# An attention and expert-layer kernel on one core: the softmax shift follows its scores by two query groups, the maxima go through TensorE in f16, and the output side moves by a group

## The reference

```
h   = layernorm(x)
q, k, v = h Wq + bq, h Wk + bk, h Wv + bv            # 16 heads of 16
s   = q.k / 4 + q.rel_emb[r - l + 511]  # 1024 x 1024 per head
x   = x + layernorm(softmax(s) v Wo + bo)
h   = layernorm(x)
w   = top 2 of softmax(h router_W + router_b), made to sum to 1
x   = x + layernorm(h base_W + base_b + shared + sum_e w_e B_e(A_e h))
```

## Time and profile before

| what | value |
|---|---|
| median of three runs | 6504.95 us (6501.69 to 6511.04) |
| profiled execution, its own time | 6501.09 us |
| its span, first to last instruction | 6499.3 us |
| mean granted TensorE clock, share of full | 0.99 |
| PE, weight loads, DVE, ACT, POOL busy | 95%, 89%, 77%, 48%, 56% |

### The profile page before, as it was taken

One profiled execution on the slowest core, in us unless ns is written; L12 is line 12 of the kernel. 1 busy time (PEld: TensorE's weight loads), 2 busy tenths in 40 slices (PEclk: granted clock), 3 DMA queues, 4 the chain that ended last, 5 costly groups with the idle time before them and its releaser, 6 DMA issues.

```text
span 6499.3 us, 408509 instructions
## 1 busy us (share of the span) xinstructions
PE 6203.9 (95%) x178176; PEld 5783.0 (89%) x178176; DVE 5036.1 (77%) x10289; ACT 3134.0 (48%) x5145; POOL 3640.9 (56%) x4707
## 2 busy tenths in 40 slices
PE   5999999999999999999999999999999999999997
PEld 4999899999999999999999999899999999998997
DVE  3777777777787777777777777777777777777776
ACT  2444444444444444444444444444444444444444
POOL 5555555555565555555555555555555555555555
PEclk8999999999999999999999999999999999999998
DMA  3111121111212112121111211112111121211210
GB/s 86 37 44 50 37 58 37 51 45 35 58 36 59 35 35 61 35 60 33 42 56 35 60 36 48 45 39 58 35 52 43 35 58 38 59 35 33 62 35 27
DMA packets 570089, 296.73 MB, mean 46 GB/s; under 512 B 384176, under 2 KB 534688, under 8 KB 568624
## 3 DMA queue, kind: packets, MB, share of 16 engines
q1 hardware_dynamic: 568624, 272.86, 15.2%
HBM read 184.46 MB, written 88.60 MB: 42 GB/s over the span
## 4 chain that ended last, share of the span: by engine, by line
PE 75%; DVE 15%; issue 6%; DVEq 3%; POOLq 1%; POOL 0%; SPq 0%; ACT 0%; DMA 0%
PE sc L665 19%; PE sc L681 13%; PE sc L660 11%; PE pw L691 11%; DVE r L960 6%; PE pm L672 6%; PE pm L712 4%; PE pw L698 4%; PE pw L712 4%; DVE nm L969 3%; DVE ceq L1008 2%; DVEq L971 2%; DVE y2n L926 1%; DVE dm L983 1%; PE pm L703 1%
## 5 line engine op out<-in xcount | busy, mean ns | idle before, releaser
L960 DVE TRANSPOSE_TENSOR_REDUCE r<-sc 128x32 f32<-128x1024 f32 x2048 | 2547.5, 1244 | 49.2 <-PE sc L665 48.3
L665 PE MATMUL sc<-rm,tw 96*128 96x32 f16 x65536 | 2288.9, 176 | 58.1 <-issue 58.1
L845 ACT ACTIVATE prob<-sc 128x1024 f32<-128x1024 f32 x2048 | 2095.7, 1023 | 237.9 <-PE sc L681 173.7
L665 PEld LDWEIGHTS sc<-rm,tw 96*128 96x128 f16 x65536 | 1976.9, 97 | 64.7 <-issue 64.3
L660 PE MATMUL sc<-qm,ks 96*128 96x64 f16 x32768 | 1635.2, 193 | 29.9 <-DMA ks<-qk_s 15.1
L969 DVE TENSOR_REDUCE nm<-pm 16x32 f16<-16x256 f32 x2048 | 840.5, 410 | 932.2 <-PE pm L672 931.4
L660 PEld LDWEIGHTS sc<-qm,ks 96*128 96x128 f16 x32768 | 1380.8, 98 | 105.7 <-issue 35.2
L681 PE MATMUL sc<-nmm,pick 128*128 128x64 f16 x32768 | 1305.7, 194 | 1.4 <-DVE nmm L972 1.4
L681 PEld LDWEIGHTS sc<-nmm,pick 128*128 128x128 f16 x32768 | 1150.9, 98 | 126.9 <-issue 103.2
L691 PE MATMUL pw<-prob,vs 128*32 128x128 f32 x32768 | 1110.2, 276 | 100.2 <-DVE nm L969 89.9
L691 PEld LDWEIGHTS pw<-prob,vs 128*32 128x32 f32 x32768 | 835.2, 110 | 158.5 <-DVE nm L969 119.8
(11 more groups left out here) (129 smaller groups left out, 5753.9 us busy)
## 6 DMA issues: line engine op xcount, KB each, us to landing
raw<-qk_s SPq DMA_DIRECT2D x774, 64.0 KB, 2.5
tw<-tw_s SPq DMA_DIRECT2D x512, 72.0 KB, 2.0
v_s<-vpad SPq DMA_DIRECT2D x136, 256.0 KB, 3.4
vs<-v_s SPq DMA_DIRECT2D x64, 512.0 KB, 3.7
ks<-qk_s SPq DMA_DIRECT2D x384, 64.0 KB, 2.4
xin<-x SPq DMA_DIRECT2D x138, 128.0 KB, 2.1
qk_s<-qkh SPq DMA_DIRECT2D x272, 64.0 KB, 1.7
qk_s<-qkl SPq DMA_DIRECT2D x272, 64.0 KB, 1.6
```

The lines of the kernel that those rows point to most:

```text
L665: last = mm(out3[:, :, 2 * k:2 * k + 2], tw[:, jp, u:u + P], rm[:, i, k, :, :], start=False, stop=False, skip_group_check=True)
L845: A(prob[:, jp % 2, :, :, i * IW:(i + 1) * IW], sc[:, 2 * buf:2 * buf + 2, :].rearrange("p c (h i) -> p c h i", i=IW), ACT.Exp).then_inc(s ...
L960: v.tensor_reduce(r1[:, :], sc[:, 2 * buf:2 * buf + 2, :].rearrange("p c (h i) -> p (c h) i", i=IW), axis=AX.X, op=ALU.max, apply_transpos ...
```

## The change

`LAG = 2` is new. In group `g` all that concerned group g-1 now concerns g-2, and the order on TensorE changes: first `transpose_max` of g-2, then `wide`, then the wait for `s_nmr`, `mixed`, the small `nm` matmul (when k is 2), and then scores of key block 0, the shift of g-2, scores of key block 1. On VectorE `spread` is that of g-2 and `maxima` that of g-1; on ScalarE the exp is that of g-2. The buffers remain three.

`r1` becomes f16 with 144 columns, of which 32 hold maxima; `transpose_max` is now a plain f16 matmul with 128 columns of `r1` as weights and a 128-column identity as the moving operand. Its output has 128 rows, of which VectorE reads 16. `nm` gets 128 rows, the unused ones zero, and its transpose has a place of its own in `pm`.

`wide` moves by a group: `transpose_parts` from k=3 to k=0 of the next stage, the projection's products from k=0 to k=1, `pv` from k=1 and k=2 to k=2 and k=3. `mixed` moves its transposes of `xn1` from g=0 to g=1 and of `o` from g=8 to g=9. ScalarE's copies move with them, and VectorE's `dm` goes from g=1 to g=3 and `o` from g=7 to g=8.

```diff
+LAG = 2
-        r1 = sb("r1", [P, 2 * H])
-        nm = sb("nm", [H, 2, P], f16)
+        r1 = sb("r1", [P, H + P], f16)
+        nm = sb("nm", [P, 2, P], f16)
...
-                    last = nc.tensor.transpose(p_max[:, c * P:(c + 1) * P], r1[:, c * H:(c + 1) * H], ident[:, :])
+                    last = mm(p_max[:, c * P:(c + 1) * P], r1[:, c * H:c * H + P], ident16[:, :], start=True, stop=True)
...
             def wide(t, n, g, att, proj, a):
-                if k and (a if jp == 0 else att):
-                    pj = (jp - 1) % NJP
-                    if k == 1:
-                        pe.wait_ge(s_exp, t * NG + g - 1)
...
-                        pv(pj, 0)
-                    elif k == 2:
-                        pv(pj, 1).then_inc(s_pv, 1)
-                    else:
-                        transpose_parts(t * NJP + jp - 1)
-                if k == 0 and jp < 3 and proj:
+                if k == 0 and (a if jp < 2 else att):
+                    transpose_parts(t * NJP + jp - 2)
+                if k == 1 and jp < 3 and proj:
...
+                if k >= 2 and (a if jp == 0 else att):
+                    pj = (jp - 1) % NJP
+                    if k == 2:
+                        pe.wait_ge(s_exp, t * NG + NI * jp)
...
+                        pv(pj, 0)
+                    else:
+                        pv(pj, 1).then_inc(s_pv, 1)
             def tile(t, n, att, proj, a, b, ph=None):
...
-                    old = a if g == 0 else att
+                    old = a if g < LAG else att
+                    count = t * NG + g - LAG + 1
+                    if read is not None:
+                        pe.wait_ge(*read)
+                    if k == 3 and (a if jp == 0 else att):
+                        pe.wait_ge(s_nmt, t * NJP + jp)
+                    if old:
+                        transpose_max(count)
+                    wide(t, n, g, att, proj, a)
+                    if old:
+                        pe.wait_ge(s_nmr, count)
+                    read = mixed(t, g, a, b)
+                    if k == 2 and (a if jp == 0 else att):
+                        mm(p_nm, nm[:, (jp - 1) % 2, :], ident16[:, 0:H], start=True, stop=True).then_inc(s_nmtp, 1)
...
                         scores(g, 0, buffer(ph, g))
-                    if read is not None:
-                        pe.wait_ge(*read)
                     if old:
-                        transpose_max(t * NG + g)
+                        shift(buffer(ph, g - LAG), count)
                     if att:
                         scores(g, 1, buffer(ph, g)).then_inc(s_scores, 1)
-
-                    wide_first = k == 1 or g in (0, 8)
-                    if wide_first:
-                        wide(t, n, g, att, proj, a)
-                    if old:
-                        pe.wait_ge(s_nmr, t * NG + g)
-                    read = mixed(t, g, att, a, b)
-                    if not wide_first:
-                        wide(t, n, g, att, proj, a)
-                    if old:
-                        shift(buffer(ph, g - 1), t * NG + g)
...
-                if g == 7 and a:
+                if g == 8 and a:
                     dve.wait_ge(s_osum, t)
...
-                        spread((g - 1) % NG, t * NG + g)
-                    if att:
-                        maxima(buffer(ph, g), t * NG + g + 1)
+                    if a if g < LAG else att:
+                        spread((g - LAG) % NG, t * NG + g - LAG + 1)
+                    if a if g < LAG - 1 else att:
+                        maxima(buffer(ph, g - LAG + 1), t * NG + g - LAG + 2)
```

More of the change, by code:

```diff
@@ L61, in sandwich_kernel @@
         ident = sb("ident", [P, P])
-        ident16 = sb("ident16", [H, H], f16)
+        ident16 = sb("ident16", [P, P], f16)
         pick = sb("pick", [P, H // 2, P], f16)
@@ L184, in sandwich_kernel @@
         pm = ctx.enter_context(nc.psum_tensor("pm", [P, 512], f32))
-        p_max = pm[0:H, 0:2 * P]
+        p_max = pm[:, 0:2 * P]
         p_n = pm[:, 2 * P:3 * P]
         p_t = pm[:, 2 * P:4 * P]
+        p_nm = pm[:, 4 * P - H:4 * P]
         s_const = sem("s_const")
@@ L503, in _ @@
             g.memset(nmm[:, :, :], 0.0)
+            g.memset(nm[:, :, :], 0.0)
+            g.memset(r1[:, :], 0.0)
             pool.drain()
@@ L510, in _ @@
             keep(ident[:, :], ALU.is_equal, 0, [[-1, P]], 1)
-            keep(ident16[:, :], ALU.is_equal, 0, [[-1, H]], 1)
+            keep(ident16[:, :], ALU.is_equal, 0, [[-1, P]], 1)
             half_h = H // 2
@@ L717, in both, with mixed @@
                 return [(lambda i, c=c: lhs[:, i, c, cols], lambda j, c=c: rhs[:, j, c, :]) for c in range(2)]
[L719 to L728, removed]
+            def mixed(t, g, a, b):
+                if g == 1 and b:
                     pe.wait_ge(s_xn1, t - 1)
@@ L736, in mixed @@
                     return s_hf, t - 1
-                if g == 8 and a:
+                if g == 9 and a:
                     pe.wait_ge(s_o, t)
@@ L758, in wide @@
                 jp, k = divmod(g, NI)
[L759 to L776 removed]
+                if k == 0 and (a if jp < 2 else att):
+                    transpose_parts(t * NJP + jp - 2)
+                if k == 1 and jp < 3 and proj:
+                    if a if jp < 2 else att:
                         pe.wait_ge(s_part, t * NJP + jp - 1)
@@ L792, in wide @@
                         product(pw[:, 0:D], *both(xT2, w_v2)).then_inc(s_vp, 1)
+                if k >= 2 and (a if jp == 0 else att):
+                    pj = (jp - 1) % NJP
+                    if k == 2:
+                        pe.wait_ge(s_exp, t * NG + NI * jp)
+                        pe.wait_ge(s_vs[pj], batch_of(t - 1 if jp == 0 else t) * 16 + 16)
+                        if proj and jp < 3:
+                            pe.wait_ge((s_xT, s_qkf, s_vf)[jp], n + 1)
+                        else:
+                            pe.wait_ge(s_part, t * NJP + jp - 1)
+                        pv(pj, 0)
+                    else:
+                        pv(pj, 1).then_inc(s_pv, 1)
             def tile(t, n, att, proj, a, b, ph=None):
@@ L849, in before @@
             def before(g, t, ph):
-                pg = (g - 1) % NG
-                exp(pg, buffer(ph, g - 1), t * NG + g, (t - 1 if g == 0 else t) * NJP + pg // NI - 1)
+                pg = (g - LAG) % NG
+                exp(pg, buffer(ph, g - LAG), t * NG + g - LAG + 1,
+                    (t - 1 if g < LAG else t) * NJP + pg // NI - 1)
             def tile(t, n, att, proj, a, b, ph=None):
@@ L859, in tile @@
                     old = a if jp == 0 else att
-                    if k == 1 and old:
+                    if k == 2 and old:
                         act.wait_ge(s_nmtp, stage + 1)
@@ L864, in tile @@
                             act.wait_ge(s_dm, t)
-                        copy(nmt[:, pj, :], p_n[:, 0:H]).then_inc(s_nmt, 1)
-                    if g == 0 and b:
+                        copy(nmt[:, pj, :], p_nm).then_inc(s_nmt, 1)
+                    if k == 0 and (a if jp < 2 else att):
+                        act.wait_ge(s_ott, stage)
+                        if jp == 2 and a:
+                            act.wait_ge(s_wp, t)
+                        copy(parts[:, (jp - 2) % NJP, :, :],
+                             pw[:, :].rearrange("p (h d) -> p h d", d=32)[:, :, 0:17]).then_inc(s_part, 1)
+                    if g == 1 and b:
                         act.wait_ge(s_x1Tp, t - 1)
@@ L880, in tile @@
                         copy(y20[:, :], p_t).then_inc(s_y20, 1)
-                    if g == 2 and a:
+                    if g == 4 and a:
                         act.wait_ge(s_dm, t)
@@ L886, in tile @@
                         A(eg[:, :], lg[:, :], ACT.Exp, bias=nlm[:, 0:1], accum_out=gsum[:, :]).then_inc(s_eg, 1)
-                    if k == 2 and old:
+                    if k == 3 and old:
                         act.wait_ge(s_pv, stage + 1)
                         copy(ot[:, :, :].rearrange("p c i -> p (c i)"), pw[:, :]).then_inc(s_ot, 1)
[L891 to L897, removed]
+                    if g == 1 and proj:
                         act.wait_ge(s_xTp, n + 1)
                         copy(xT[:, :, :].rearrange("p c i -> p (c i)"), pw[:, 0:2 * P]).then_inc(s_xT, 1)
-                    if g == 4 and proj:
+                    if g == 5 and proj:
                         act.wait_ge(s_qkp, n + 1)
@@ L903, in tile @@
                         copy(qkf[:, :, :].rearrange("p e i -> p (e i)"), pw[:, :]).then_inc(s_qkf, 1)
-                    if g == 8 and proj:
+                    if g == 9 and proj:
                         act.wait_ge(s_vp, n + 1)
@@ L907, in tile @@
                         copy(vf[:, :], pw[:, 0:D]).then_inc(s_vf, 1)
-                    if g == 8 and a:
+                    if g == 9 and a:
                         act.wait_ge(s_oTp, t)
                         copy(oT[:, :, :].rearrange("p c i -> p (c i)"), p_t).then_inc(s_oT, 1)
-                    if a if g == 0 else att:
```

(3 more changed lines are left out.)

8 lines of the change are left out of this document (4 added, 4 removed).

## The result

The changed kernel takes 6714.91 us (median of 4 runs, 6703.08 to 6721.85) against 6503.32 us (4 runs): a ratio of 1.0321, 95% interval 1.0303 to 1.0339. It is slower by 3.2%; forecast were 2.5% and 6670 us, with a range up to 6820.

The account below looks back on a forecast made before the run. TensorE's program, its work plus its waits, was taken to set the pace. The terms summed to +1.39 us a tile, rounded down to 1.3; times 128, +166 on 6505 gave about 6670 us, range 6480 to 6820.

Parts of the forecast that it names:

- The transposes, -1.76: On TensorE, sixteen transpose pairs a tile would cost 0.11 us each instead of 0.22, saving 1.76 us a tile.
- The wait for the reduction, +2.05: TensorE waits for VectorE's reduction, 0.78 us from the transposes' start, badly covered at k=0, g=1, g=13: 2.05 us a tile more.
- The wait for the exp, +1.8: At k=2 `pv` waits for ScalarE's exp until 1.27 us after the shift, losing 0.45 four times: 1.8 us a tile.
- The late spreads of before, -1.2: Old stalls behind late reductions vanish: 0.8 us at group 6, 0.2 at group 15, 0.2 for one more place.
- VectorE's pace, +0.4 and +0.4: VectorE late in g=9 after the `o` product, 0.4 us a tile; shared-port slowness of `nmm` in short groups, 0.4 more.
- Overlapping issue stalls, -0.3: Issue stalls in TensorE's 32-column scores, 0.45 us a tile, would partly catch up during semaphore waits: 0.3 us a tile saved.
- rival 3: VectorE sets the pace, its lateness passed on between groups: 1.4 us more a tile, about 6850 us; chance 0.13.
- Rivals 1 and 2: TensorE's new waits covered better than reckoned, about 6375 us, chance 0.13; or parity, about 6500 us, chance 0.08.
- rival 4: Wide f16 transposes no cheaper, 0.22 us a pair: 1.76 us more a tile, about 6895 us; chance 0.04.

Follow-up runs that it names:

- both repairs of the changed order: Changed kernel, waiting for the reduction only where its bank is written, with the tile's waits ahead of the transposes: 6677.38 us, ratio 1.026.

## Why the prediction was right, by its steps

- **The transposes, -1.76.** The price of 0.11 a pair is right. The weight-load figure of the Trainium skill ("TensorE: Matmul & The Clock Gate", section "LDWEIGHTS (loading the stationary operand)"), which would have left the pair as dear as before, does not hold here as a pace: the trace has 0.11 from start to start for two loads and two matmuls. A load by itself is shown as 0.095 us long; the loads overlap. As a part of the sum the term stands, because the waits were reckoned behind a pair of 0.11. As a statement of what the edit is worth it does not: 127 us in the changed order and 153 in the old one, where 1.76 a tile is 225.
- **The wait for the reduction, +2.05.** Right: 0.78 from the transposes to the scores in group 13, and short groups of 2.53 where 2.54 was worked out. Taking it away gave much less than its size, as there is a second wait behind it.
- **The wait for the exp, +1.8.** Right in place and near in size: 0.46 in group 10, 0.44 regained in groups 2 and 14. Group 10's was partly covered by another wait, so removing all four gave 1.37.
- **The late spreads of before, -1.2.** Group 6's 0.8 is gone. In the old order with cheaper transposes it grows to 0.9. The other two show in the table: groups 7 and 15 have the same work on TensorE, and so have 14 and 2. Before, group 15 was 0.28 longer than group 7 and group 2 was 0.17 longer than group 14; after, the pairs are equal. That group 2's was a late spread is not shown: it goes with the cheaper transposes alone (2.96 in both groups).
- **VectorE's pace, +0.4 and +0.4.** `o` in group 9 is right: 3.15 against 2.74 of work and wait. The term for VectorE slowed by GpSimd came out near its size by luck. It was reckoned from slow `nmm` in the short groups, but those last 2.53 and `nmm` became faster in the mean (281 ns for 341). The 0.52 stands in group 5, a long one, behind `lg` at 1.40 us beside GpSimd's product. Holding that product back gave 0.35 of it and cost more in group 7.
- **Overlapping issue stalls, -0.3.** The size is right, the reason was not. 58.1 to 12.3 us inside the scores is -0.36 a tile, of which 20.7 us, 0.16 a tile, comes back before the transposes. But the stalls were never spread over the tile for a wait to cover: there were 68 in the whole run, and 48.2 of the 58.1 us fell behind the 41 passes of the back edge.
- **What was missing:** group 0, +0.43 a tile or 55 us. The prediction has no term for the waits at the start of a tile. They are the same waits, but they had 0.48 us of shift queued ahead of them before, and now they stand behind a wait that has emptied the queue. With it the sum of 1.39 becomes 1.82, against 1.72 measured.

So the two new waits and their sizes were foreseen; that the total came within 45 us also took luck, since one term was missing and another had the right size from the wrong place.

The rivals: VectorE does set the pace in places (groups 5 and 9, and 7 when things are moved), but the short groups end at 2.53 by TensorE's own waits, so rival 3 did not decide. Rivals 1 and 2 are out by the waits measured, and rival 4 by the pair at 0.11.

## What to carry to other kernels

Read for each wait what covers it in time from the producer's start, not how many steps lie between: a lag of two groups gave less cover than one, because the consumer moved to right behind the producer. When an edit has a part that shortens work and a part that reorders, run the parts alone: here one gives 2.3% and the other takes 5.2%. A cheaper instruction in front of a wait gives nothing at that place, as in groups 2, 6, 10 and 14, so look at the waits behind it first.

## What the runs showed of the hardware beyond expectation

`nmm`, 16 by 64 values in f16, takes 0.18 us in the median and once in the changed kernel 2.28 us. Timeline, VectorE and GpSimd, around it:

```profile
3031.66 2.28 DVE L971 TENSOR_TENSOR nmm<-nm,mask_h 16x64 f16<-16x64 f16 x1
...
3030.96 0.72 POOL L643 TENSOR_TENSOR res<-y2n,x1b 128x256 f32<-128x256 f32 x1
3031.65 1.15 POOL L536 TENSOR_TENSOR qm<-raw,mask_q 96x512 f16<-96x512 f16 x1
3032.76 1.14 POOL L537 TENSOR_TENSOR rm<-raw,mask_r 96x512 f16<-96x512 f16 x1
```

It ends within 0.05 us of GpSimd's second mask product, and TensorE stood idle 1.31 us before the shift. It had also been idle for 0.57 and 0.28 us in the 5 us before that. Its clock then fell. Windows of 2 us (PE, weight loads, DVE, ACT, POOL, granted clock, DMA share, GB/s):

```profile
3032.00:3034.00 2.00, 0.69 (x26) 0.59 (x23) 2.00 (x2) 0.66 (x2) 2.00 (x3) 1.00 0.23 73
3034.00:3036.00 2.00, 1.80 (x50) 1.52 (x54) 1.51 (x2) 1.02 (x1) 1.86 (x4) 0.73 0.31 78
3036.00:3038.00 2.00, 2.00 (x40) 1.54 (x33) 1.83 (x5) 0.15 (x1) 0.86 (x2) 0.50 0.61 138
```

At 0.50, the 1.2 GHz level, a half of `pv` took 1.94 us instead of 1.08, and with the scores behind it the low stretch cost about a microsecond. Whether the stall of 1.31 us alone brought the clock down is not shown. This is rare: from 160 us on, 14 of 650 windows of 10 us show a clock below full in the changed kernel, 10 of 628 before, and 31 of 646 in the kernel with both repairs of the changed order, most of them behind the back edge.
